# A four-layer graph network in one kernel: constants of the edge comparison in PSUM, another batch order, and the last stages merged

## The reference

```python
x = layernorm(x + L0(x))   # three GCN convolutions (edge weights), relu between, then @ Wl
x = layernorm(x + L1(x))   # two SAGE convolutions (mean over neighbours)
x = layernorm(x + L2(x))   # encoder, five steps of message passing + GRU, decoder:
#   for w in conv_w:
#       gi = segment_sum((h @ w)[src], dst) @ wih.T + bih;  gh = h @ whh.T + bhh
#       r = sigmoid(ir + hr); z = sigmoid(iz + hz); n = tanh(i_n + r * h_n)
#       h = (1 - z) * n + z * h
#   out = sigmoid(relu(relu(h) @ dec_w1.T + dec_b1) @ dec_w2.T + dec_b2)
x = layernorm(x + L3(x))   # one GCN convolution, no edge weights: segment_sum(norm * (x@W)[src]) + b
```

## Time and profile before

| what | value |
|---|---|
| median of 3 runs | 5748.14 us (5744.3 to 5749.56) |
| the profiled execution's own time | 5746.37 us |
| its span, first to last instruction | 5744.6 us |
| PE busy | 4803.0 us, 84% |
| POOL busy | 2567.7 us, 45% |
| DVE busy | 1751.7 us, 30% |
| ACT busy | 1204.8 us, 21% |
| mean granted TensorE clock | 0.892 |

### The profile page before, as it was taken

One profiled execution on the slowest core, in us unless ns is written; L12 is line 12 of the kernel. 1 busy time (PEld: TensorE's weight loads), 2 busy tenths in 40 slices (PEclk: granted clock), 3 DMA queues, 4 the chain that ended last, 5 costly groups with the idle time before them and its releaser, 6 DMA issues. The chain is left out here.

```text
span 5744.6 us, 79088 instructions
## 1 busy us (share of the span) xinstructions
PE 4803.0 (84%) x25665; PEld 2581.3 (45%) x25665; DVE 1751.7 (30%) x3228; ACT 1204.8 (21%) x2507; POOL 2567.7 (45%) x1704
## 2 busy tenths in 40 slices
PE   3555555496299999999999998999999999997796
PEld 3555555242145444444454544444444444443343
DVE  9999999200000100010050303103030120303413
ACT  5555556100011111111120102112020110202200
POOL 4888888888888888888885000000000000000100
PEclk7555555697699999999999999999999999999897
DMA  9999983487399999999989785775858668582474
GB/s 352 358 354 353 351 238 52 119 240 220 49 303 302 270 300 289 301 273 299 288 235 298 242 294 185 224 254 182 299 174 271 215 222 268 172 299 74 146 261 135
DMA packets 717086, 1401.96 MB, mean 244 GB/s; under 512 B 268372, under 2 KB 356264, under 8 KB 691880
## 3 DMA queue, kind: packets, MB, share of 16 engines
q1 hardware_dynamic: 483832, 1346.10, 69.9%
q0 software_dynamic: 225216, 0.70, 7.6%
q10 hardware_dynamic: 7920, 53.79, 2.4%
HBM read 1160.09 MB, written 240.25 MB: 244 GB/s over the span
## 5 line engine op out<-in xcount | busy, mean ns | idle before, releaser
L837 PE MATMUL psum<-arena 128*128 128x512 f16 (+3 forms) x14014 | 3683.0, 424 | 299.4 <-issue 171.9
L837 PEld LDWEIGHTS psum<-arena 128*128 (+2 forms) x14014 | 1671.9, 124 | 2245.1 <-issue 1113.7
L548 POOL DMA_INDIRECT W_adj<-arena x782 | 1289.3, 1649 | 257.1 <-issue 239.1
L548 POOL DMA_INDIRECT C_adj<-arena x782 | 1213.9, 1552 | 240.1 <-issue 240.0
L680 POOL TENSOR_TENSOR arena<-arena 128x512 f32 (+1 forms) x13 | 22.1, 1700 | 1811.7 <-DVE arena L1172 1811.7
L427 DVE TENSOR_SCALAR_CACHE_REDUCE arena<-arena 128x2048 bf16<-128x2048 f32 (+7 forms) x392 | 709.5, 1875 | 0.6 <-issue 0.6
L497 PE MATMUL psum<-arena 128*128 (+1 forms) x6664 | 224.6, 167 | 482.7 <-DVE arena L449 459.4
L497 PEld LDWEIGHTS psum<-arena 128*128 128x128 bf16 x6664 | 213.7, 104 | 499.2 <-issue 450.3
L1356 DVE COPY arena<-psum 128x512 f32<-128x512 f32 (+1 forms) x39 | 23.2, 653 | 1353.5 <-PE psum L847 1159.4
L270 ACT ACTIVATE arena<-arena 128x1024 bf16<-128x1024 f32 (+7 forms) x392 | 298.5, 773 | 401.3 <-DVE arena L427 387.8
L1358 DVE TENSOR_SCALAR arena<-psum,arena 128x512 f32<-128x512 f32 x30 | 21.9, 748 | 1038.9 <-PE psum L837 1038.9
(11 more groups left out here) (233 smaller groups left out, 2594.5 us busy)
## 6 DMA issues: line engine op xcount, KB each, us to landing
arena<-C_adj SPq DMA_DIRECT2D x784, 384.0 KB
arena<-W_adj SPq DMA_DIRECT2D x294, 768.0 KB
arena<-C_adj SPq DMA_DIRECT2D x392, 512.0 KB
arena<-W_adj SPq DMA_DIRECT2D x147, 1024.0 KB
arena<-C_adj SPq DMA_DIRECT2D x392, 288.0 KB
arena<-W_adj SPq DMA_DIRECT2D x147, 576.0 KB
W_adj<-arena SPq DMA_DIRECT2D x12, 6400.0 KB
W_adj<-arena SPq DMA_DIRECT2D x12, 6144.0 KB
```

Of the source, the lines that this page charges most:

```text
L548: return pool.indirect_dma_start(table, bass.IndirectOffsetOnAxis(idx[:, t:t + 1], 0), values[:, t:t + 1], None, compute_op=ALU.add)
L837: ins = pe.matmul(psum[:, bank + b, 0:width], lhs, ring[:, slot, b * BANK:b * BANK + width], start=begin and part == 0, stop=False, skip_g ...
```

## The change

1. `compare` reads its constants from PSUM: `psRamp` and `psUpto` (bank 2) and `psW` (banks 4 and 5), all float32.
2. The batch order becomes 0, then groups 2, 4, 1, 3 (plus 4g), and at the end 45, 47, 46, 48.
3. The small DVE work that makes `flight` and `ready` moves behind the first batch's merge (`conflicts`). SP writes all zeros of `W_adj` before those of `C_adj`.
4. `gru 4` and `decode` become one stage `out`, written out unit by unit: GRU products of unit j+1, then the decoder of unit j, with the first sweep's chunks of unit j-2 between them.
5. `last` is gone as a stage. The final product, norm and output of a block of columns run in the next sweep of `out`, one unit after each lap of 8 chunks; the three units of the last sweep run behind it. ACT issues the output DMAs.

```diff
+ORDER = [0] + [4 * g + u for g in range((NB - 5) // 4) for u in (2, 4, 1, 3)]
+ORDER += [b for u in (0, 1) for b in range(len(ORDER) + u, NB - 1, 2)] + [NB - 1]
...
+    psRamp, psUpto = psum[:, 2, 0:P], psum[:, 2, P:2 * P]
+    psW = psum[:, 4:6, :].rearrange("p a b -> p (a b)")[:, 0:TILES]
...
-        for z in range(BLOCKS):
-            at_, width = z * BANK, block_width(z)
-            for table, of, zeroed in ((W_rows, zero, w_zeroed), (C_rows, z16, c_zeroed)):
+        for table, of, zeroed in ((W_rows, zero, w_zeroed), (C_rows, z16, c_zeroed)):
+            for z in range(BLOCKS):
+                at_, width = z * BANK, block_width(z)
...
-            dve.tensor_tensor(high, rampb[:, 0:CHUNKS].unsqueeze(1).to_broadcast([P, TB, CHUNKS]),
+            dve.tensor_tensor(high, psRamp[:, 0:CHUNKS].unsqueeze(1).to_broadcast([P, TB, CHUNKS]),
...
-            dve.tensor_tensor(ohl, rampb.unsqueeze(1).to_broadcast([P, TB, P]),
+            dve.tensor_tensor(ohl, psRamp.unsqueeze(1).to_broadcast([P, TB, P]),
...
-            dve.tensor_tensor(Et[:, slot, 0:half, :], near, upto.unsqueeze(1).to_broadcast([P, half, P]), ALU.mult)
+            dve.tensor_tensor(Et[:, slot, 0:half, :], near, psUpto.unsqueeze(1).to_broadcast([P, half, P]), ALU.mult)
...
-            dve.tensor_tensor(weighted, high, w[:, b * TB:(b + 1) * TB].unsqueeze(2).to_broadcast([P, TB, CHUNKS]),
+            dve.tensor_tensor(weighted, high, psW[:, b * TB:(b + 1) * TB].unsqueeze(2).to_broadcast([P, TB, CHUNKS]),
...
+            if b == 0:
+                conflicts()
...
-    return stages + [("gru", STEPS - 1, None), ("decode", None, (False, "ln", True)), ("last", None, None)]
+    return stages + [("out", None, (False, "ln", True))]
...
+                    if name == "out" and j >= 2:
+                        pe.wait_ge(s["dec_read"], j - 1)
+                        pe.wait_ge(s["dec_mid"], j - 1)
...
+            def last_product(j):
+                if j >= 2:
+                    pe.wait_ge(s["products_read"], last.read + j - 1)
+                for c in range(chunks_of(j)):
+                    ins = pe.matmul(psum[:, LAST_BANKS[j % 2], c * D:(c + 1) * D],
+                                    sum_fm[:, (j * UC + c) * P:(j * UC + c + 1) * P], wt["L3W"], start=True, stop=True)
+                ins.then_inc(s["products"], 1)
...
+            def decoded(j):
+                pe.wait_ge(s["state_set"], j + 1)
+                pe.wait_ge(s["gates_set"], 2 * base.gates + 2 * min(j + 2, UNITS))
+                pe.matmul(psum[:, 5, :], wt["D1T"], unit(h_fm, j), start=True, stop=True).then_inc(s["dec_in"], 1)
+                spell((j - OUT_LAG) * UC + 1)
+                pe.wait_ge(s["dec_mid"], j + 1)
+                for c in range(UC):
+                    ins = pe.matmul(psum[:, 4, c * D:(c + 1) * D], own_in[:, j % 2, c * P:(c + 1) * P],
+                                    wt["D2T"], start=True, stop=True)
+                ins.then_inc(s["dec_out"], 1)
+
+            if name == "out":
+                products(0, 0)
+                for j in range(UNITS):
+                    if j + 1 < UNITS:
+                        products(j + 1, 0)
+                    spell((j - OUT_LAG) * UC)
+                    decoded(j)
+                    spell((j - OUT_LAG) * UC + 2)
+                    spell((j - OUT_LAG) * UC + 3)
+                for c in range((UNITS - OUT_LAG) * UC, CHUNKS):
+                    spell(c)
...
+                    if name == "out":
+                        for j in blocks_of(sweep - 1):
+                            for u in range(LAP):
+                                chunk(lap * LAP + (u + 1), u, sweep, 16 * lap + 16 * (laps + 1))
+                            pe.wait_ge(s["sum_dve"], base.sum_dve)
+                            pe.wait_ge(s["sum_act"], base.sum_act)
+                            last_product(j)
+                            lap += 1
+                    with pe.Fori(lap, LAPS) as i:
```

More of the change, by code:

```diff
@@ L558, in stage_list, with last_layer, blocks_of, chunks_of @@
     stages += [("gru", n, (False, 1, False)) for n in range(STEPS - 1)]
-    return stages + [("gru", STEPS - 1, None), ("decode", None, (False, "ln", True)), ("last", None, None)]
+    return stages + [("out", None, (False, "ln", True))]
+def last_layer(stages):
+    last = Bases()
+    for stage in stages:
+        last.advance(*stage)
+    last.units = units_before(stages, len(stages))
+    return last
+def blocks_of(sweep):
+    first, n, _ = SWEEPS[sweep]
+    return range(first, first + n)
+def chunks_of(j):
+    return UC if j < UNITS - 1 else CHUNKS - UC * (UNITS - 1)
 class Bases:
@@ L647, in run_layers @@
     stages = stage_list()
+    last = last_layer(stages)
+    result = h_fm.rearrange("p (c f) -> p c f", f=D)
     def unit(ap, j):
@@ L979, in scalar @@
             wide = feeds is not None and feeds[0]
-            norm = (name, arg) in (("gcn", 2), ("enc", 1)) or name in ("decode", "last")
+            norm = (name, arg) in (("gcn", 2), ("enc", 1)) or name == "out"
             base_units = units_before(stages, k)
@@ L985, in lead @@
             def lead(j, q):
[L987 removed]
+                if name in ("gcn", "sage", "enc"):
                     if not isinstance(j, int) or j >= 2:
@@ L1063, in encoded, with decoded @@
                                scale=up[:, 1:2]).then_inc(s["hi_set"], 1)
-            if name == "enc":
+            def decoded(j):
+                act.wait_ge(s["dec_in"], j + 1)
+                if j >= 2:
+                    act.wait_ge(s["dec_out"], j - 1)
+                act.activation(own_in[:, j % 2], psum[:, 5, :], ACT.Relu, bias=col["db1"]).then_inc(s["dec_mid"], 1)
+                act.wait_ge(s["dec_read"], j + 1)
+                act.activation(work, work, ACT.Sigmoid).then_inc(s["dec_set"], 1)
+                root(j)
+            if name == "out":
+                lead(0, 0)
+                main(0, 0)
+                for j in range(UNITS):
+                    if j + 1 < UNITS:
+                        lead(j + 1, 0)
+                        main(j + 1, 0)
+                    decoded(j)
+            elif name == "enc":
                 lead(0, 0)
@@ L1091, in scalar @@
                     base.selfs += feeds[2]
+                    if name == "out" and sweep:
+                        for j in blocks_of(sweep - 1):
+                            last_unit(j)
                     if not wide:
@@ L1176, in vector, with last_unit @@
             norm_at = [None]
+            def last_unit(j):
+                dve.wait_ge(s["products"], last.products + j + 1)
+                ps = bank_nm(LAST_BANKS[j % 2])
+                for c in range(chunks_of(j)):
+                    ins = dve.scalar_tensor_tensor(out=work[:, c, :], in0=ps[:, c, :],
+                                                   scalar=dinv_c[:, j * UC + c:j * UC + c + 1],
+                                                   in1=x_nm[:, j * UC + c, :], op0=ALU.mult, op1=ALU.add)
+                ins.then_inc(s["products_read"], 1)
+                dve.wait_ge(s["products_read"], last.read + j + 1)
+                norm_at[0] = last.norms + j + 1
+                normalise(lambda c: result[:, j * UC + c, :], chunks_of(j))
+                dve.wait_ge(s["unit_set"], last.units + j + 1)
             def two_parts(of, j, scale=LN_SCALE):
@@ L1345, in vector @@
                         dve.tensor_copy(gates, psum[:, 7, 0:3 * D])
+                    if name == "out" and sweep:
+                        if sweep == 1:
+                            dve.wait_ge(s["kept"], kept + UNITS)
+                        for j in blocks_of(sweep - 1):
+                            last_unit(j)
                     base.used += CHUNKS
```

242 lines of the change are left out of this document (110 added, 132 removed).

## The result

The changed kernel takes **5504.86 us** (median of five runs, 5502.16 to 5508.78), against 5746.48 us for the kernel before, measured beside it (five runs). The ratio is 0.9579, 95% interval 0.9566 to 0.9592: faster by 242 us. The forecast was 5484 with a range of 5450 to 5532, so it lies 21 us above the point and inside the range. The profiled execution took 5502.16 us, its span is 5500.3.

What follows compares the result with a forecast made beforehand. The prediction took DVE to bound the build, POOL's adds the gated sweeps, and PE most of the rest. Terms -115 - 93 + 9 - 65 = -264 gave 5482 us, 5484 on the median; range 5450 to 5532.

Steps and rivals of the forecast that it cites:

- front, to the end of gru 3: Up to gcn 2's last sweep: earlier POOL gates and new batch order gain 115 us, bounds 100 and 135.
- gru 4 and decode to out: Merging both stages: 195 us against 288, 93 us gained, bounds 77 and 97.
- last products in the sweeps: Ten units' final products between chunks of the three sweeps: +9 us, bounds 7 and 14.
- the tail: Behind the last sweep: three units, about 16 us, stay of 81; -65 us, bounds -60 and -67.
- W_adj takes 1478: POOL's W_adj adds at C_adj's pace: 1478 us instead of 1567, 89 us earlier, bounds 80 and 95.
- If its gate is later, the slower DVE costs nothing: First stage's third sweep: PE's wait for POOL covers a build 52 to 67 us longer.
- PE's cold start: gcn 2's last sweep: after waiting 32 us PE starts cold, +2 us.
- PSUM constants: Build: PSUM inputs in five operations per batch bring W_adj adds 89 us earlier; DVE takes 52 to 67 us more.
- Rival A: POOL's adds don't get faster; the front gains 28 instead of 115: 5571 us; 6%.
- Rival B: Merged stage doesn't overlap; PE, DVE and ACT wait in a ring, 18 us a step: 5536 us; 8%.
- Rival D: C_adj gate doesn't bind because W_adj's adds gain more; the front gains 149: 5448 us; 4%.
- rival C: Slow DVE reads of PSUM make the build set everything, slower than before; 5858 us at 10 us more per batch; 2%.

Runs made afterwards that it cites:

- e8: The changed kernel with the last three batches of C_adj left out (output differs): 5468.8 us.
- e3: The changed kernel with the batch order as before the change (1, 3, 0, 2 in each group of four): 5528.4 us.
- e5: The changed kernel with the first W_adj sweep's loads held until the adds up to add 560 have landed: 5490.6 us.
- e2: The changed kernel with the triangle alone back in SBUF as bf16: 5489.4 us.
- e1: The changed kernel with the build on VectorE as before the change, ramp, triangle and weights in SBUF: 5568.6 us.
- e6: The changed kernel with the VectorE build as before, except that the 2.28 us comparison takes its ramp from PSUM: 5497.2 us.
- e10: The changed kernel with one more 0.69 us VectorE operation per unit's decoder part in stage out: 5506.2 us.
- e11: The changed kernel with all 49 first-sweep chunks of stage out behind the 13 units instead of between them: 5579.6 us.
- e7: The changed kernel with all 13 units of the last layer behind the last sweep, none inside the sweeps: 5538.9 us.

## Why the prediction was right, and where it was off

**The sum, term by term** (profiled spans, 5744.6 to 5500.3, so -244.3 against -264 forecast):

| term | forecast | measured |
|---|---|---|
| front, to the end of gru 3 | -115 (-100 to -135) | -92.5 (5197.7 to 5105.2) |
| gru 4 and decode to out | -93 (-77 to -97) | -95.5 (287.7 to 192.2) |
| last products in the sweeps | +9 (7 to 14) | +9.0 (178.4 to 187.4) |
| the tail | -65 (-60 to -67) | -65.3 (80.8 to 15.5) |

**The front is the term that was mis-sized**, by 22 us and past its own bound of 100. No other term made up for it; the total stayed inside its range because the range is 82 us wide. Its mechanism held: adds at the pace of the C_adj adds, both gates set by POOL, a wait of 30.8 us (forecast 32) before gcn 2's last sweep, e8 showing its price and e3 that it takes up a part of what the order gives. The failed step is "W_adj takes 1478": it took 1501. The adds themselves were no slower than those of C_adj (1211.1 against 1213.5 us in sum), but pauses over 1.3 us add up to 50 us in the W_adj half and 14 in the C_adj half, where I had allowed for 7 more. 17.7 of the missing 23 us are the pause at add 561 (18.0 instead of 0.3), and the rest is mostly the pauses of 4 to 7 us at adds 113, 225 and 337 of the build. With the pause at 561 gone and all else kept (e5) the time is 5490.6, 7 us off the point of the forecast. Both gates moved by these 23 us: the third sweep came at 1462 instead of 1438, the last C_adj add at 3041 instead of 3018.

**"If its gate is later, the slower DVE costs nothing"** is the sentence behind it that was wrong, and the most instructive one. It named the cover (PE's idle time before the third sweep) and the cover was there: 51.9 us of it. But the end of the build also sets when the ring's first loads are issued, nine of 128 x 2048 float32 (1 MB each). Issued from 1101.8 on, their burst meets add 561, from 1047.3 on (e2) it doesn't. e2 takes the 54 us of VectorE back and is 15 us faster, e5 keeps them and moves the burst, and is 14 us faster. The profile before did hold the pattern: POOL's pauses at adds 113, 225 and 337 (up to 4.45 us, 112 adds apart), with the one at 561 hardly visible (1.3 us, at 1225). These are the adds behind the first and the last of these pauses:

```profile
319.43 1.55 POOL L548 DMA_INDIRECT W_adj<-arena  x1 [4.44 <-issue]
...
1225.37 1.55 POOL L548 DMA_INDIRECT W_adj<-arena  x1 [1.34 <-issue]
```

The prediction says that POOL "issues adds without a pause"; I had read the adds' durations and not the gaps between them.

The prediction's 2 us for PE's cold start rest on 0.417 us a matmul, which no row gives; but the second sweep, now without a wait ahead of it (clock 1.00), took 126.0 us, as that sum has it.

**PSUM constants.** Rival A (the adds don't get faster) is refuted by e1: 64 us net, paid in full. But the gain wasn't where I had put it, in all five operations: e6 shows that the 2.28 us comparison alone brings nearly all of it, and e2 that the two bf16 products didn't need their PSUM operand. On POOL's side an add in L437 waits for its end; on VectorE's side a running add never held an operation up (2284 ns with one under way, 2286 without). The Trainium skill's page "SBUF — State Buffer", section "SBUF: two separate sides", says of the port pair that a DVE operation with two SBUF inputs and a GpSimd operation that reads SBUF share, that whichever "starts first gets the pair for the whole instruction; the other fully blocks". The rows agree with it where VectorE started first, and not where the add did. The fixed cost of a PSUM operand that I had bounded at 0.06 us isn't there: 969 ns with and 970 ns without it for the 784-element comparison (the second row is e6's):

```profile
L438 DVE TENSOR_TENSOR arena<-arena 128x784 f32<-128x784 bf16 x46 | 44.6, 970 | 0.0
```

**Stage out.** 14.0 to 14.2 us a step were forecast, 13.81 came, and 195 for the stage against 192.2. The sum over PE was right. The remark that VectorE is full too was wrong: its 13.7 us held waits; it is busy 10.8 of 13.81 us (62.3 of 80), and e10 puts 0.69 us more on it for nothing. Rival B (a ring of waits) is refuted at full PE load. e11 shows how near it was: the round trip is 13.66 us at the lower clock, so interleaving hides it rather than shortens it.

**Last layer.** Both numbers came as forecast. e7 divides the 65 us into 42 for the early units and 23 for the new form, which I hadn't told apart; and 9 of the 42 are given back in the sweeps.

**Rival D** (the C_adj gate doesn't bind) and **rival C** (PSUM reads set the build) didn't come; the build ended at 1100, inside 1098 to 1114.

**A version that beats both** is e2: the change with the triangle left in SBUF, 5489.4 us. e5, at 5490.6, can't be told from it.

## What to carry to other kernels

When an edit is priced at nothing because another engine's idle time covers it, ask also which transfers its end starts, and what they run into: here 54 us that nobody waited for moved a burst of loads onto a queue's weak moment and cost 15. Move to PSUM the one long two-SBUF-operand operation that other work runs into, and leave short bf16 ones where they are fast. For an engine that sets the pace by many equal instructions, read the gaps between them as well as their durations, since each nanosecond counts once per instruction.

## What the runs showed of the hardware

- POOL's indirect adds of 128 values come every 1.55 + 0.30 us, but pause behind the first add of every seventh batch: behind adds 113, 225, 337, 449, 561 and 673 of W_adj, and behind the adds of the same numbers of C_adj (895, 1007 and so on of all). From 673 to 895 are 222 adds and not 224, since W_adj's last batch has 14. So whether a count or the place in the program sets them isn't shown.
- Such a pause lasts until the adds in flight have landed (156 of 156 places, see e5). After 449, where few were in flight, it is 0.3 to 1.0 us in all kernels; the others take up to 9 us. The one after 561 took 13.9 to 19.6 us in all eight kernels whose first row loads began 38 to 43 us before it, against 0.3 to 2.0 in the five where they began 94 us or more before it (the kernel before, e1, e2, e6) or just as it came (e5). e5 shows that the burst makes it long.
- An add that starts while VectorE runs an operation with two SBUF operands ends 1.42 us behind that operation (if more than some 0.13 us of it are left); the operation isn't slowed by an add that is under way.
- 28 small loads issued on POOL's queue before the first add made each of 1564 adds 12 to 14 ns longer (1547 to 1559 ns median). The cause is open.
- A bf16 product of 1024 elements takes 0.68 us from SBUF and 1.21 us with one float32 operand in PSUM; no run parts the operand's type from its place. A comparison with float32 output takes the same either way.
